# Graph layers on one core: queries before values, three scales for x, tiles split by groups, products of ones at the start

## The reference

```python
# layer 0
q = x @ Wq.T + bq;  k = x @ Wk.T + bk;  v = x @ Wv.T + bv
a = q @ k.T / sqrt(512) + adj + adj
x = layernorm(x + softmax(a) @ v)
# layer 1, W1 is 512 x 128, W2 is 128 x 512
h = relu(adj @ (x @ W1) + b1)
x = layernorm(x + adj @ (h @ W2) + b2)
```

## Time and profile before

| | us |
|---|---|
| runs: median of 3 (lowest, highest) | 1917.98 (1917.07, 1918.20) |
| profiled execution, its own time | 1917.4 |
| its span, first to last instruction | 1915.4 |
| TensorE busy in it | 1894.9 (99%) |
| DVE, ACT, POOL busy | 1074.8, 857.9, 114.5 |

### The profile page before, as it was taken

How to read it: one execution, slowest core, us unless ns; L and a number is a source line. 1 busy time by engine, 2 the same in 40 slices (tenths; PEclk the granted TensorE clock), 3 DMA queues, 4 the chain that set the end, 5 groups by cost and what they waited for, 6 DMA issues and landing times.

```text
span 1915.4 us, 26409 instructions
## 1 busy us (share of the span) xinstructions
PE 1894.9 (99%) x9252; PEld 885.7 (46%) x9252; DVE 1074.8 (56%) x2049; ACT 857.9 (45%) x1837; POOL 114.5 (6%) x207
## 2 busy tenths in 40 slices
PE   7999999999999999999999999999999999999998
PEld 3444444444444444444444444444444454444445
DVE  7875666666666666666666666666666620002334
ACT  5654464555555555555555555555445511011112
POOL 0000000000000000000000000000000000002334
PEclk9999999999999999999999999999999999999999
DMA  8563599999999999999999999999999999979996
GB/s 282 116 141 86 131 236 224 232 228 223 227 224 223 233 228 229 225 225 224 227 229 225 228 227 226 230 222 224 227 226 237 218 345 387 387 290 390 394 394 248
DMA packets 799526, 465.29 MB, mean 243 GB/s; under 512 B 644641, under 2 KB 652321, under 8 KB 799137
## 3 DMA queue, kind: packets, MB, share of 16 engines
q1 hardware_dynamic: 789888, 446.82, 94.0%
q10 hardware_dynamic: 9504, 16.79, 2.4%
HBM read 223.09 MB, written 92.01 MB: 165 GB/s over the span
## 4 chain that ended last, share of the span: by engine, by line
PE 93%; DMA 2%; DVE 2%; issue 1%; POOL 1%; ACT 1%; SPq 0%; POOLq 0%; DVEq 0%; ACTq 0%
PE bank L526 14%; PE bank L528 14%; PE bank L527 14%; PE bank L621 11%; PE bank L623 11%; PE bank L622 11%; PE bank L739 5%; PE bank L740 5%; PE bank L738 5%; DMA tsp<-gT 1%; POOL tsp L1491 1%; DMA adj_in<-in_L_gnn_Wv 1%; DMA xv<-in_x 0%; DVE sc L1066 0%; DVE ring L1077 0%
## 5 line engine op out<-in xcount | busy, mean ns | idle before, releaser
L879 ACT ACTIVATE tsp<-ring,sc 128x512 f16<-128x512 f32 x249 | 179.7, 722 | 601.5 <-DMA tsp<-tsp 600.8
L1246 DVE SCALAR_TENSOR_TENSOR ring<-bank,sc,adj_in 128x512 f32<-128x512 f32 x256 | 192.2, 751 | 389.2 <-PE bank L528 383.7
L621 PE MATMUL bank<-xv,tsp 128*128 128x512 f16 x1024 | 388.1, 379 | 1.8 <-DMA tsp<-gT 1.8
L526 PE MATMUL bank<-xT,gT 128*128 128x512 f16 x1024 | 388.1, 379 | 0.0
L527 PE MATMUL bank<-xT,gT 128*128 128x512 f16 x1024 | 388.1, 379 | 0.0
L528 PE MATMUL bank<-xT,gT 128*128 128x512 f16 x1024 | 388.1, 379 | 0.0
L622 PE MATMUL bank<-xv,tsp 128*128 128x512 f16 x1024 | 388.1, 379 | 0.0
L623 PE MATMUL bank<-xv,tsp 128*128 128x512 f16 x1024 | 388.1, 379 | 0.0
L1077 DVE SCALAR_TENSOR_TENSOR tsp<-adj_in,s_a,tsp 128x512 f16<-128x512 f32 x248 | 184.8, 745 | 53.9 <-ACT tsp L887 53.2
L1077 DVE SCALAR_TENSOR_TENSOR tsp<-ring,sc,tsp 128x512 f16<-128x512 f32 x249 | 185.7, 746 | 2.6 <-ACT tsp L879 2.6
L869 ACT ACTIVATE ring<-ring,bias 128x512 f32<-128x512 f32 x256 | 180.9, 707 | 8.8 <-DVE bias L1263 8.8
(11 more groups left out here) (224 smaller groups left out, 2124.5 us busy)
## 6 DMA issues: line engine op xcount, KB each, us to landing
xv<-at_dram SPq DMA_DIRECT2D x66, 1024.0 KB, 11.6
adj_in<-in_adj SPq DMA_DIRECT2D x256, 256.0 KB, 3.4
at_dram<-tsp SPq DMA_DIRECT2D x248, 256.0 KB, 3.2
xT<-at_dram SPq DMA_DIRECT2D x21, 1024.0 KB, 16.3
adj_in<-at_dram SPq DMA_DIRECT2D x18, 1024.0 KB, 11.1
xv<-in_x SPq DMA_DIRECT2D x8, 1024.0 KB, 11.2
g_dram<-tsp SPq DMA_DIRECT2D x32, 256.0 KB, 3.7
gT<-g_dram SPq DMA_DIRECT2D x32, 256.0 KB, 3.7
```

What stands on the lines that cost most here:

```text
L526: pe.matmul(dst, ah, bh, start=(i == 0), stop=False)
L621: pe.matmul(dst, ah, vh, start=(kb == 0 and j == 0), stop=False)
L879: act.activation(p_split(e)[:, 0:BANK], p, ACT.Copy, scale=col[f"p_up{batch(TW * kb)}"]).then_inc(a_p, 1)
L1246: dve.scalar_tensor_tensor(t, s_bank[s % S_BANKS][:, :], col[f"k_l{batch(s // KB)}{batch(TW * (s % KB))}"], adj_in[:, s % AR, :], ALU.mult ...
```

## The change

- Wq and Wk come in two transfers each: the first quarter of both, then the rest. x group 0 comes ahead of Wv; bv and groups 2 to 5 behind the first four transposes, 6 and 7 in step 0.
- TensorE does nine products of ones while nothing has landed. M is computed piece by piece over all four banks, so that the first pieces need only the first quarter. The Wv transposes come behind M and the small products.
- DVE does both partial sums first, then scale 0 of x, the maxima of M among the first x tiles, M's scale and low parts, and only then Wv's scale and low parts.
- The loop takes two steps at a time: two queries, then two values; queries(t) goes with values(t). A product of queries waits for all four tiles of its group. Values have two banks.
- x has three scales: group 0, group 1, groups 2 to 7. All sums are on ACT.
- The four tiles of the next group are split at step t = 0, 8, 12, ... together, and tiles 8 to 11 at step 6, with `g_hi(t)` behind the second of them.
- g is stored one group earlier, and loading g waits for the last group sum, since the sums now use g's place as scratch.

```diff
-SP_GROUPS = 4
+BATCHES = 3
+BATCH_STARTS = (0, XG, FIRST)
+WARM_UP = 9
...
-V_BANKS = 4
+V_BANKS = 2
...
-    return 0 if t < FIRST else 1
+    return min(t // XG, BATCHES - 1)
 
 
 def x_tiles_at(t):
 
 
-    if t < FIRST - 3:
-        return [t + XS + 1] if t + XS + 1 < FIRST else []
-    if t <= FIRST:
-        return {FIRST - 3: [FIRST, FIRST + 1], FIRST - 2: [FIRST + 2], FIRST - 1: [FIRST + 3],
-                FIRST: [FIRST + 4, FIRST + 5]}[t]
-    return [t + XS + 1] if t + XS + 1 < NT else []
+    first = FIRST if t == FIRST - 2 else t + XG if t % XG == 0 and t + XG != FIRST else NT
+    return list(range(first, first + XG)) if first < NT else []
...
-        x_junk = tsp[:, 7, :].bitcast(mybir.dt.float8e4)
+        x_junk = gT[:, 0, :].bitcast(mybir.dt.float8e4)
...
-            return bank[n % 2] if n < NT - XG else bank[6 + n % 2]
+            return bank[n % 2] if n < XG else bank[6 + n % 2]
...
         def _(sp):
-            sp.dma_start(wq_raw, wq.rearrange("(p k) d -> p k d", k=KD)).then_inc(d_wq, 16)
-            sp.dma_start(wk_raw, wk.rearrange("(p k) d -> p k d", k=KD)).then_inc(d_wk, 16)
-            sp.dma_start(wv_raw, wv.rearrange("(k p) d -> p k d", p=P)).then_inc(d_wv, 16)
+            wq_rows, wk_rows = (w.rearrange("(p k) d -> p k d", k=KD) for w in (wq, wk))
+            sp.dma_start(wq_raw[:, 0:1, :], wq_rows[:, 0:1, :]).then_inc(d_w0, 16)
+            sp.dma_start(wk_raw[:, 0:1, :], wk_rows[:, 0:1, :]).then_inc(d_w0, 16)
+            sp.dma_start(wq_raw[:, 1:KD, :], wq_rows[:, 1:KD, :]).then_inc(d_wr, 16)
+            sp.dma_start(wk_raw[:, 1:KD, :], wk_rows[:, 1:KD, :]).then_inc(d_wr, 16)
             x_tiles = x.rearrange("(t p) d -> p t d", p=P)
 
             def load_x(i):
                 sp.dma_start(xv[:, XG * i:XG * (i + 1), :], x_tiles[:, XG * i:XG * (i + 1), :]).then_inc(d_x[i], 16)
 
-            for i in range(X_FIRST):
-                load_x(i)
-            sp.dma_start(bv_row, bv.rearrange("(o d) -> o d", o=1).broadcast_to([P, D])).then_inc(d_bv, 16)
-            for i in range(X_FIRST, SP_GROUPS):
-                load_x(i)
+            load_x(0)
+            sp.dma_start(wv_raw, wv.rearrange("(k p) d -> p k d", p=P)).then_inc(d_wv, 16)
+            load_x(1)
...
 
             for t in range(XS):
                 transpose_x(t)
-            load_x(SP_GROUPS)
-            transpose_x(XS)
-            for i in range(SP_GROUPS + 1, NT // XG - 1):
+            sp.dma_start(bv_row, bv.rearrange("(o d) -> o d", o=1).broadcast_to([P, D])).then_inc(d_bv, 16)
+            for i in range(X_FIRST, X_FIRST + 4):
                 load_x(i)
             for t in range(NT):
                 for q in x_tiles_at(t):
                     transpose_x(q)
                 if t == 0:
-                    load_x(NT // XG - 1)
+                    for i in range(X_FIRST + 4, NT // XG):
+                        load_x(i)
                 if t == XG:
                     sp.dma_start(w1_raw.rearrange("p (k f) -> p k f", k=KD), w1.rearrange("(k p) f -> p k f", p=P)).then_inc(d_w1, 16)
                     sp.dma_start(b1_c[:, :], b1.rearrange("(p o) -> p o", o=1)).then_inc(d_b1, 16)
                     sp.wait_ge(p_pre, KD + 3)
                     for s in range(2):
                         load_adj(s)
-                if t % XG == 0 and t >= 2 * XG:
-                    store_g(t // XG - 2)
+                if t % XG == 0 and t >= XG:
+                    store_g(t // XG - 1)
                 if t == 3 * XG:
+                    sp.wait_ge(a_xs, NT // XG)
                     load_gt(0)
                 if t >= 3 * XG and t % 2:
                     s = 2 + (t - 3 * XG) // 2
                     if s < 9:
                         load_adj(s)
-            store_g(NT // XG - 2)
...
+            pe.wait_ge(g_set, 1)
+            for i in range(WARM_UP):
+                pe.matmul(bank[7][:, 0:P], ones, ones, start=True, stop=True)
+            pe.wait_ge(d_w0, 16 * 2)
+            for e in range(KD):
+                if e == 1:
+                    pe.wait_ge(d_wr, 16 * 2)
+                for k in range(KD):
+                    last = pe.matmul(m_bank[k][:, :], wq_raw[:, e, P * k:P * (k + 1)], wk_raw[:, e, :],
+                                     start=(e == 0), stop=(e == KD - 1))
+                    if e == KD - 1:
+                        last.then_inc(p_pre, 1)
...
+            pe.wait_ge(d_wv, 16)
+            pe.wait_ge(g_id, 2)
+            wv_transposes(0)
+            wv_transposes(1)
+            pe.wait_ge(v_gb, 2)
+            wv_transposes(2)
+            pe.wait_ge(a_bias, 1)
+            wv_transposes(3)
...
             def values(t):
-                pe.wait_ge(d_xt[t % XS], 16 * (t // XS + 1))
-                if t == 0:
-                    pe.wait_ge(a_wv, KD)
-                    pe.wait_ge(v_wv, KD)
-                if t == 2:
-                    pe.wait_ge(v_gb, 2)
-                if t == 3:
-                    pe.wait_ge(a_bias, 1)
                 if t >= V_BANKS:
                     pe.wait_ge(v_vf, t - V_BANKS + 1)
-                product(v_bank[t % V_BANKS][:, :],
-                        [(xt_block(0, k, P * t, P), xt_block(1, k, P * t, P), wvT[:, 0, k, :], wvT[:, 1, k, :])
-                         for k in range(KD)]).then_inc(p_v, 1)
+                if t % XG == 0:
+                    for i in range(XS):
+                        pe.wait_ge(d_xt[i], 16 * (t // XG + 1))
+                for k in range(KD):
+                    if t == 0:
+                        pe.wait_ge(a_wv, k + 1)
+                        pe.wait_ge(v_wv, k + 1)
+                    last = terms(v_bank[t % V_BANKS][:, :], xt_block(0, k, P * t, P), xt_block(1, k, P * t, P),
+                                 wvT[:, 0, k, :], wvT[:, 1, k, :], k == 0, k == KD - 1)
+                last.then_inc(p_v, 1)
             def queries(n):
                 g, kk = divmod(n, KD)
-                if n == 0:
-                    pe.wait_ge(a_m, KD)
-                    pe.wait_ge(v_m, KD)
+                if kk == 0:
+                    for i in range(XS):
+                        pe.wait_ge(d_xt[i], 16 * (g + 1))
                 if n >= 2:
                     pe.wait_ge(a_gf, n - 1)
...
-            for t in range(NT):
+            for t in range(0, NT, 2):
+                if t < NT - XG:
+                    queries(t)
+                    queries(t + 1)
                 values(t)
-                if t >= XG:
-                    queries(t - XG)
+                values(t + 1)
...
             group_sum(0)
-            act.wait_ge(v_sc, 1)
-            wv_hi(0)
-            wv_hi(1)
-            group_sum(1)
-            wv_hi(2)
-            wv_hi(3)
             for t in range(XS):
                 xt_hi(t)
-            group_sum(2)
-            xt_hi(XS)
-            group_sum(3)
+            group_sum(1)
             act.wait_ge(p_pre, KD + 3)
             act.activation(c_row, bank[7][:, :], ACT.Copy).then_inc(a_bias, 1)
             act.wait_ge(v_sm, 1)
             for k in range(KD):
                 m_hi(k)
+            act.wait_ge(v_sc, 1)
+            for k in range(KD):
+                wv_hi(k)
+            group_sum(2)
             for t in range(NT):
+                for i, q in enumerate(x_tiles_at(t)):
+                    if i == 2:
+                        g_hi(t)
+                    xt_hi(q)
+                if t % 2 == 0 and t < NT - XG:
+                    if not x_tiles_at(t):
+                        g_hi(t)
+                    g_hi(t + 1)
                 v_hi(t)
-                for q in x_tiles_at(t):
-                    xt_hi(q)
-                if t >= XG:
-                    g_hi(t - XG)
-                if SP_GROUPS + t < NT // XG:
-                    group_sum(SP_GROUPS + t)
+                if t + 3 < NT // XG:
+                    group_sum(t + 3)
...
-                dve.wait_ge(g_ar, 2 + 2 * b)
-                if b == 1:
-                    link(dve.tensor_reduce(col["mx_x1"], x_all[:, :], AX, ALU.max))
+                dve.wait_ge(g_ar, (1, 2, 6)[b])
+                if b == BATCHES - 1:
+                    link(dve.tensor_reduce(col[f"mx_x{b}"], x_all[:, :], AX, ALU.max))
...
+            partial(part_u, wq_raw, bk_c, range(KD))
+            partial(part_g, wk_raw, bq_c, range(KD))
             link(dve.tensor_tensor(bqk[:, :], bq_c[:, :], bk_c[:, :], ALU.mult))
             dve.tensor_reduce(col["c0p"], bqk[:, :], AX, ALU.add).then_inc(v_part, 1)
             x_scale(0)
+            dve.wait_ge(d_wv, 16)
+            wv_max(0)
             xt_lo(0)
             xt_lo(1)
+            m_max(0)
             xt_lo(2)
+            m_max(1)
+            xt_lo(3)
+            m_max(2)
+            m_max(3)
+            dve.tensor_reduce(col["st_m"], cols("m0", "m3"), AX, ALU.max).then_inc(v_st, 1)
             dve.wait_ge(p_pre, KD + 2)
             dve.tensor_scalar(gb_c[:, :], bank[6][:, 0:KD], LOGIT, None, ALU.mult).then_inc(v_gb, 1)
```

(52 more changed lines are left out.)

140 lines of the change are left out of this document (37 added, 103 removed), and 3 rows, old and new, of the table names.

## The result

| | before | after |
|---|---|---|
| median, us | 1917.51 (1915.5 to 1918.71, 7 runs) | 1924.09 (1923.34 to 1925.48, 7 runs) |
| profiled execution, us | 1917.4 | 1924.11 |
| its span, us | 1915.4 | 1922.2 |
| first logits matmul, us | 185.87 | 192.76 |
| span behind that mark, us | 1729.5 | 1729.4 |

The ratio after to before is 1.0034 [1.0024, 1.0044]. 1924.2 was predicted. The last two rows of the table say where to look: all of the loss is there when the first logits start, and none comes behind it.

The account below looks back on a forecast made before the run. TensorE was taken as the bound, with only the opening to win or lose. Start -3.15, waits +10.6 less 2.8, clock +1.7 put first logits 6.3 us later, at 192.2: 1924.2 us, range 1915.5 to 1928 for 8 in 10.

Parts of the forecast that it names:

- the start: Opening: queries(0) start at 24.62 us, 3.15 us ahead of the first value product of before at 27.77.
- wait (4): Queries(8) wait 6.65 us, to 76.6, for tiles 8 to 11, which need the third x scale and group 7's sum.
- the clock: TensorE's clock falls to half rate behind the wait at queries(8), costing 1.7 us; bounds 0 and twice 1.7.
- wait (1): Values(0) wait 1.2 us for Wv's second scale and the low parts made with it.
- wait (2): Queries(2) wait 2.3 us for g_hi(0), behind x_scale(1) and ScalarE's tiles 4 and 5.
- wait (3): Queries(4) and queries(6) wait 0.15 us each for g_hi(2) and g_hi(4), behind group sums.
- waits of now, gone: Waits of the kernel before between 27.77 us and the first logits, 2.8 us, disappear.
- rival A: No wait at queries(8), as sums and scales run ahead of the count: 1916.0 us; 0.22 with its neighbours.
- C: Rival: every wait put in is hidden, for instance by a quicker early DVE block: 1912 us; chance 0.06.
- B: Rival: the wait at queries(8) comes but the clock does not fall: 1922.5 us; chance 0.14.
- D: Rival: queries later still, by transposes that land late or a second fall of the clock: 1929 us; chance 0.07.
- E: Rival: the weight product M still waits for all of Wk, everything behind 3.4 us later: 1927.6 us; chance 0.03.

Follow-up runs that it names:

- e1: The kernel after without the nine products of ones: 1925.13 us, ratio to before 1.0040.
- e2: The kernel after with VectorE making the second x scale before it waits for Wv's high parts: 1921.61 us, ratio to before 1.0020.
- e3: The kernel after without the sums of x groups 5 to 7, the third scale coming from groups 2 to 4: 1921.90 us, ratio 1.0023.
- e10: The kernel after with early second x scale and first partial-sum terms, sums respread, x loads issued together, tiles 8 to 11 split at step 5: 1916.52 us.
- e13: e10 with x groups 6 and 7 loaded behind the transposes of tiles 4 to 7 again: 1915.44 us, ratio to before 0.9988.
- e5: The kernel after with 8 filler matmuls ahead of the wait of queries(2): 1929.31 us in a single run.
- e12: The kernel after, unedited, timed and profiled once more: 1924.15 us, ratio to before 1.0033.
- e4: The kernel after with 20 filler matmuls into an unused bank ahead of the wait of queries(8): 1924.14 us, ratio to before 1.0037.

## Why the prediction was right

It was right in sign, size and place: 1924.2 against 1924.09, first logits 192.2 against 192.76. That the medians agree to 0.1 us is luck: the start was 0.7 us later, wait (4) 1.1 shorter and the clock cost 1.4 more than forecast, and another profile of the same kernel has the first logits at 194.21. Its terms, with what the profile after has for each:

| term | forecast | measured |
|---|---|---|
| start, queries(0) | 24.62, -3.15 | 25.34, -2.4 |
| wait (1), values(0) | 1.2 | 1.2 |
| wait (2), queries(2) | 2.3 | 2.2 |
| wait (3) | 2 x 0.15 | none |
| wait (4), queries(8) | 6.65, at 76.6 | 5.55, at 77.48 |
| clock | 1.7, behind (4) | 1.7 behind (2), 1.4 behind (4) |
| waits of now, gone | -2.8 | -2.8 |
| first logits | +6.3 | +6.9 |

**The start.** 0.7 us late by one step: I let the rest of Wk land at 8.55 as now, but VectorE started its partial sums at 9.30 against 8.65, and the whole file moved with it. M ended at 19.6, not 19.0, for the same reason. That M is not what is waited for held in the kernel after, but with 0.6 us to spare by e1, where I had counted 1.8 (M done at 19.0, the last maximum begun at 20.8) and had not looked at the first maximum.

**Waits (1) and (2)** came as the file of VectorE gave them, within 0.1 us. e2 shows wait (2) to be the place of x_scale(1) and nothing else: moved, the wait is gone.

**Wait (4)** is shown twice. The third scale is late by ScalarE's file: the forecast had it at 67.95 and it was 68.25. Anything that took time off the road to it, e2's earlier start or e3's missing sums, brought queries(8) ahead by the same amount, 2.3 and 2.45 us. e10 and e13, which move the sums into idle time of ScalarE and split tiles 8 to 11 a step earlier, have queries(8) at 70.5 and 70.7, 7 us earlier, with waits of 0.5 and 2.2 us. So rival A's ground, that ScalarE had the room, was true of another order of the same work.

**The clock** was right as a sum and wrong in how it comes. I put one fall behind wait (4); the first profile had a second behind wait (2), my outer bound, which moved the end of values(7) from 70.2 to 71.9 and so took 1.7 us out of wait (4). Waits and clock together were 12.1 us where the forecast has 12.3 (its four waits add up to 10.45; the 10.6 in its sum is 0.15 too much). A fall ahead of a wait that is fixed by another engine costs nothing (e5 and e12 beside the first profile), one behind it costs in full.

**The rivals.** A (1916.0) and C (1912) fell at once, with queries(8) at 77.48. B, the wait without the clock, would be 1922.5: e4's profile is the only one near it in the trace, and its median is not. D had two arms. Late transposes didn't come: they landed in 3.1 to 3.4 us. A second fall of the clock did, but ahead of wait (4), where it cost nothing. E is excluded by M's start at 5.46.

By the Trainium skill, "TensorE: Matmul & The Clock Gate", section "Part 4: PE-mode transpose", transposes don't count as activity for the clock, and queries(0) behind the 16 transposes might have started at half rate. They did not here: the query matmuls from 25.34 are 0.22 apart. With transposes of 2.06 us and a wait of 1.68 us ahead of them, no run here shows the rule at work.

## What to carry to other kernels

When work is put in front of an engine that is the bound, follow to its end the one-file chain that feeds each later product: an earlier start of 2.4 us was worth nothing while one bound over all of x stood at the end of another engine's file. A wait taken away gives back only what it moves in the file that ends the next wait (2.0 of 3.9 us in e2, none of 2.3 in e13). A sum placed early waits for its load with everything behind it, so place work by when its data land, and let no bulk load stand ahead of the small transfers that the bound engine needs next.
